# Two heads per maximum and exponential, and a shorter table of steps, in a four-layer attention and expert kernel on one core

## The reference

```python
x = _L0_conv_ref(x, ...)                     # one-head attention over 256 positions, 16 channels wide
x = x + _L1_conv_ref(_gn(x), ...)            # group norm, 8-head attention (16 channels each), projection
t = _to_tokens(x)
t = t + _L2_attn_ref(_ln_t(t))               # softmax(x x^T) x
t = t + _L2_ffn_ref(_ln_t(t), ...)           # 8 experts of 512, all of them, weighted by two probabilities
t = t + _L3_attn_ref(_ln_t(t), ...)          # 8 heads, RoPE, window of 32 keys back
t = t + _L3_ffn_ref(_ln_t(t), ...)           # shared expert and 2 of 8 routed experts of 64
```

## Time and profile before

| | us |
|---|---|
| median of 3 runs (lowest, highest) | 787.24 (785.09, 787.25) |
| the profiled execution | 783.05 |
| span of its trace | 781.3 |
| PE matmul busy | 633.1 (81%) |
| VectorE busy | 390.9 (50%) |
| ScalarE busy | 343.4 (44%) |
| GpSimd busy | 333.7 (43%) |

### The profile page before, as it was taken

The page is one execution under the profiler, slowest core; times in us unless marked ns, Lnnn a source line. Parts: engine busy times, 40 slices in busy tenths (PEclk is TensorE's granted clock), DMA queues, the critical chain, the costliest instruction groups (busy, mean ns, idle before and its releaser), DMA issues.

```text
span 781.3 us, 9513 instructions
## 1 busy us (share of the span) xinstructions
PE 633.1 (81%) x3266; PEld 324.7 (42%) x3266; DVE 390.9 (50%) x799; ACT 343.4 (44%) x544; POOL 333.7 (43%) x620
## 2 busy tenths in 40 slices
PE   7788988677888977887997869996689889757768
PEld 5565455444344442434443424442334344334422
DVE  3464441557375564674556385644675434531233
ACT  2423224136466465365455346653744634212222
POOL 2543411606174186696146685428671534200300
PEclk9997566789999999988999889999999999855789
DMA  6600000000000000000000000000000000000000
GB/s 211 146 1 1 1 1 1 0 1 1 1 0 1 1 1 1 1 0 0 2 0 2 0 1 0 1 1 1 0 0 1 1 1 14 13 1 1 0 14 13
DMA packets 10226, 8.59 MB, mean 11 GB/s; under 512 B 4026, under 2 KB 8132, under 8 KB 10180
## 3 DMA queue, kind: packets, MB, share of 16 engines
q1 hardware_dynamic: 10180, 8.00, 3.6%
HBM read 6.94 MB, written 1.05 MB: 10 GB/s over the span
## 4 chain that ended last, share of the span: by engine, by line
PE 51%; DVE 16%; POOL 14%; issue 10%; ACT 8%; DMA 0%; POOLq 0%; SPq 0%; DVEq 0%; ACTq 0%
PE bank L540 9%; PE bank L547 8%; POOL h_s L1278 4%; ACT ET L750 4%; DVE shiftpad L1015 4%; DVE z_s L1090 3%; POOL xn_l L1271 3%; PE bank L266 3%; PE bank L399 3%; PE bank L431 3%; PE bank L454 2%; PE bank L413 2%; PE bank L591 2%; PE bank L576 2%; PE bank L391 1%
## 5 line engine op out<-in xcount | busy, mean ns | idle before, releaser
L1090 DVE TENSOR_TENSOR z_s<-bank,PB 128x1024 f32<-128x1024 f32 x128 | 156.4, 1222 | 164.7 <-PE bank L540 162.6
L1278 POOL TENSOR_TENSOR h_s<-z_s 128x512 f32<-128x512 f32 x128 | 163.0, 1299 | 153.7 <-ACT z_s L809 135.4
L540 PE MATMUL bank<-XN_C,W 128*128 128x512 f32 x256 | 144.1, 646 | 34.3 <-DVE z_s L1090 33.7
L547 PE MATMUL bank<-h_s,W 128*128 128x512 f32 x256 | 145.3, 651 | 1.4 <-ACT y_s L816 1.0
L809 ACT ACTIVATE z_s<-z_s,b 128x1024 f32<-128x1024 f32 x128 | 137.2, 1141 | 11.0 <-DVE z_s L1090 10.8
L1015 DVE TENSOR_REDUCE shiftpad<-bank 128x2 f32<-128x512 f32 (+1 forms) x128 | 66.6, 583 | 53.9 <-PE bank L399 29.4
L540 PEld LDWEIGHTS bank<-XN_C,W 128*128 128x128 f32 x256 | 44.7, 199 | 101.8 <-DVE z_s L1090 79.3
L750 ACT ACTIVATE ET<-bank 128x512 f32<-128x512 f32 (+1 forms) x128 | 55.8, 522 | 57.0 <-PE bank L431 30.1
L1264 POOL TENSOR_SCALAR root_l<-mv_l 128x4 f32<-128x4 f32 x12 | 2.8, 232 | 168.8 <-DVE mv_l L1046 168.3
L547 PEld LDWEIGHTS bank<-h_s,W 128*128 128x128 f32 x256 | 44.5, 202 | 37.0 <-issue 31.4
L771 ACT COPY XN_C<-bank 128x512 f32<-128x512 f32 x16 | 9.4, 585 | 68.2 <-PE bank L266 68.1
(11 more groups left out here) (246 smaller groups left out, 961.3 us busy)
## 6 DMA issues: line engine op xcount, KB each, us to landing
W<-in_L_ffn_W_dram SPq DMA_DIRECT2D x1, 2048.0 KB, 8.7
XN_C<-in_x_dram SPq DMA_DIRECT2D x4, 256.0 KB, 3.0
out_dram<-z_s SPq DMA_DIRECT2D x4, 256.0 KB, 2.2
Wgate<-in_L_ffn_W_gate_dram SPq DMA_DIRECT2D x1, 256.0 KB, 4.2
Wup<-in_L_ffn_W_up_dram SPq DMA_DIRECT2D x1, 256.0 KB, 4.8
Wdown<-in_L_ffn_W_down_dram SPq DMA_DIRECT2D x1, 256.0 KB, 4.3
early<-in_L_conv_W_qkv_dram SPq DMA_DIRECT2D x1, 192.0 KB
early<-in_L_conv_Wd_dram SPq DMA_DIRECT2D x1, 64.0 KB, 1.9
```

Of the source, the lines that this page charges most:

```text
L540: nc.tensor.matmul(to[:, :], W1[:, f // 4, f % 4 * P:(f % 4 + 1) * P], XN_C[:, pair(g)], start=True, stop=True).then_inc(filled("u", t)[0], 1)
L547: ins = nc.tensor.matmul(bank[D_BANK][:, :], W2[:, f, :], h_s[:, t % H_RING, :], start=(f == 0), stop=(f == FT - 1)).then_inc(s_dn, 1)
L1090: nc.vector.tensor_tensor(z_s[:, t % Z_RING, :].rearrange("p (w n) -> p w n", w=2), content("u", t)[:, None, :].broadcast_to([P, 2, W]), P ...
L1278: nc.gpsimd.tensor_tensor(h_s[:, t % H_RING, :], z_s[:, t % Z_RING, 0:W], z_s[:, t % Z_RING, W:2 * W], ALU.add).then_inc(s_h, 1)
```

## The change

Banks 3 to 6 become one tensor `quad`, and banks 3 and 4 share one pair of semaphores, 5 and 6 another (`KEEPER`). S and T take both pairs before their first matmul (`take_two`) and report a pair when its second head is done. `highest` and `exps` handle a pair of heads in one instruction: 64 maxima and 64 exponentials in place of 128 and 128. There are two sets of offsets: in the expert turns (`SLOW`) S, MT, T, PV, OT stand at 0 and 2, 2 and 4, 4 and 6, 6 and 8, 9, and the second pair's maximum and exponential come a step later than the first's; outside the turns (`FAST`) at 0 and 1, 1 and 2, 1 and 2, 2 and 3, 4. Within a step PE now does MT and PV ahead of T. The turns begin at step 32, and the table has 203 steps instead of 224. In the steps before 32 the ring of banks 1 and 7 has bank 0 as a third member. `prepare_late` moves from s = 18 to s = 42, and the experts of group 2 now stand in steps 180 to 185, among the halves of images 14 and 15. The lines move: L540 is L561 in the changed kernel, L1090 is L1118, L1015 is L1042, L750 is L776, L399 is L420, L431 is L452, L454 is L475, L413 is L434, L355 is L376, L497 is L518, L516 is L537, L266 is L287.

```diff
-FF_AT = 36
+FF_AT = 32
-L0_AT = (0, 3, 6, 9)
-P1_AT = (8, 12, 30, 44)
-ATT_AT = (9, 13, 17, 21, 33, 41, 49, 57, 89, 97, 121, 129, 153, 161, 185, 189)
-TAIL_AT = (22, 30, 50, 66, 106, 138, 170, 198)
-L2_AT = (27, 37, 61, 77)
-SPREAD_AT = (35, 45, 69, 101)
+L0_AT = (0, 3, 10, 16)
+P1_AT = (7, 13, 22, 28)
+ATT_AT = (8, 10, 14, 16, 37, 45, 53, 61, 93, 101, 117, 125, 149, 157, 179, 181)
+TAIL_AT = (15, 21, 56, 72, 112, 136, 168, 186)
+L2_AT = (20, 26, 61, 77)
+SPREAD_AT = (30, 40, 72, 104)
-PREP_AT = tuple(FF_AT + FT * g + 45 for g in range(3)) + (177,)
-ROUTER_AT = (113, 145, 177, 205)
-EXPERT_AT = (172, 178, 200, 211)
-LAST = 224
-U_BANK, D_BANK, QUAD_BANK, MISC = (0,), 2, 3, (1, 7)
-XG_BANK, XU_BANK, XW_BANK = (0, 3), (4, 6), 5
+PREP_AT = (81, 109, 141, 172)
+ROUTER_AT = (118, 141, 173, 191)
+EXPERT_AT = (168, 174, 180, 196)
+LAST = 203
+U_BANK, D_BANK, QUAD_BANK, MISC, MISC_FIRST = 0, 2, 3, (1, 7), (1, 7, 0)
+KEEPER = (0, 1, 2, 3, 3, 5, 5, 7)
+SLOW = {"S": (0, 2), "MT": (2, 4), "T": (4, 6), "PV": (6, 8), "OT": 9, "later": 1}
+FAST = {"S": (0, 1), "MT": (1, 2), "T": (1, 2), "PV": (2, 3), "OT": 4, "later": 0}
+STEPS = [FAST if at < FF_AT or at > FF_AT + TURNS else SLOW for at in ATT_AT]
...
+        quad = ctx.enter_context(nc.psum_tensor("quad", [P, SLOTS, 512], F32))
...
+            def take_two(what, i, jj):
+                return fill(what, i, (QUAD_BANK + 2 * jj, QUAD_BANK + 2 * jj + 1))
...
-                to = [take("S", (i, j), QUAD_BANK + j) for j in range(SLOTS)] if a >= IMAGES else [None] * SLOTS
+                for jj in range(2):
+                    take_two("S", (i, jj), jj)
...
-                        if t == NT - 1:
-                            ins.then_inc(filled("S", (i, j))[0], 1)
+                        if t == NT - 1 and j % 2 == 1:
+                            ins.then_inc(filled("S", (i, j // 2))[0], 1)
...
-                    to = take("xg", (g, k), XG_BANK[k % 2])
+                    to = take("xg", (g, k), (0, QUAD_BANK)[k % 2 if g == GROUPS - 1 else 0])
-                    to = take("xu", (g, k), XU_BANK[k % 2])
+                    to = take("xu", (g, k), (1, 5)[k % 2] if g == GROUPS - 1 else None)
-                        to = take("xw", (g, k), XW_BANK)
+                        to = take("xw", (g, k), 7 if g == GROUPS - 1 else None)
...
-                for j in range(SLOTS):
-                    act.wait_ge(*filled("T", (i, j)))
-                    nc.scalar.activation(ET[:, i % 2 * SLOTS + j, 0:width(a)], content("T", (i, j))[:, 0:width(a)], ACT.Exp).then_inc(
-                        emptied("T", (i, j))[0], 1)
+                at = i % 2 * SLOTS + 2 * jj
+                act.wait_ge(*filled("T", (i, jj)))
+                nc.scalar.activation(ET[:, at:at + 2, 0:width(a)], quad[:, 2 * jj:2 * jj + 2, 0:width(a)], ACT.Exp).then_inc(emptied("T", (i, jj))[0], 1)
...
-                for j in range(SLOTS):
-                    dve.wait_ge(*filled("S", (i, j)))
-                    nc.vector.tensor_reduce(shiftpad[:, i % 2, :, j, HD], content("S", (i, j))[:, 0:width(a)].rearrange("p (t k) -> p t k", t=NT),
-                                            AX.X, ALU.max, negate=True).then_inc(emptied("S", (i, j))[0], 1)
+                at = slice(2 * jj, 2 * jj + 2)
+                dve.wait_ge(*filled("S", (i, jj)))
+                nc.vector.tensor_reduce(shiftpad[:, i % 2, :, at, HD].rearrange("p t j -> p j t"),
+                                        quad[:, at, 0:width(a)].rearrange("p j (t k) -> p j t k", t=NT),
+                                        AX.X, ALU.max, negate=True).then_inc(emptied("S", (i, jj))[0], 1)
...
-                if s == 18:
+                if s == FF_AT + 10:
                     prepare_late()
```

More of the change, by code:

```diff
@@ L249, in _, with fill @@
         def _(pe):
-            turns = [0]
+            turns, beat = {MISC: 0, MISC_FIRST: 0}, [0]
+            def fill(what, i, banks):
+                kept = KEEPER[banks[0]]
+                was = max(content_of[b] for b in banks)
+                if was:
+                    pe.wait_ge(bank_emptied[kept], was)
+                fills[kept] += 1
+                for b in banks:
+                    content_of[b] = fills[kept]
+                turn_of[what, i] = banks[0], fills[kept]
+                return bank[banks[0]]
             def take(what, i, b=None):
                 if b is None:
[L255 to L261, removed]
+                    ring = MISC if beat[0] >= FF_AT else MISC_FIRST
+                    turns[ring] += 1
+                    b = ring[turns[ring] % len(ring)]
+                return fill(what, i, (b,))
+            def take_two(what, i, jj):
+                return fill(what, i, (QUAD_BANK + 2 * jj, QUAD_BANK + 2 * jj + 1))
             def turn_tiles(what, i, source, to=None):
@@ L441, in values @@
                 i = a * 2 + half
-                for j in range(SLOTS):
-                    pe.wait_ge(*emptied("T", (i, j)))
+                for jj in range(2):
+                    pe.wait_ge(*emptied("T", (i, jj)))
                 if half == 0:
@@ L598, in _ @@
             for s in range(LAST):
+                beat[0] = s
                 for g in range(GROUPS):
@@ L605, in _ @@
                 for a in range(2 * IMAGES):
[L606 to L611 removed]
+                    for half in range(2):
+                        if s == ATT_AT[a] + STEPS[a]["MT"][half]:
+                            turn_shifts(a, half)
+                for a in range(2 * IMAGES):
+                    for half in range(2):
+                        if s == ATT_AT[a] + STEPS[a]["PV"][half]:
+                            values(a, half)
+                    if s == ATT_AT[a] + STEPS[a]["OT"]:
                         turn_o(a)
+                for a in range(2 * IMAGES):
+                    for half in range(2):
+                        if s == ATT_AT[a] + STEPS[a]["T"][half]:
+                            scores_turned(a, half)
                 for ap in range(2 * GROUPS):
@@ L618, in _ @@
                 for a in range(2 * IMAGES):
-                    k = s - ATT_AT[a]
-                    if k in (0, 2):
-                        scores(a, k // 2)
-                    if k in (1, 3):
-                        turn_shifts(a, k // 2)
+                    for half in range(2):
+                        if s == ATT_AT[a] + STEPS[a]["S"][half]:
+                            scores(a, half)
                 if 0 <= s - FF_AT - DOWN_LAG < TURNS:
@@ L1155, in _ @@
                 for a in range(2 * IMAGES):
-                    k = s - ATT_AT[a]
-                    if k == 8:
+                    for half in range(2):
+                        if s == ATT_AT[a] + STEPS[a]["MT"][half]:
+                            add_shift(a, half)
+                for a in range(2 * IMAGES):
+                    if s == ATT_AT[a] + STEPS[a]["OT"]:
                         scale_o(a)
@@ L1164, in _ @@
                 for a in range(2 * IMAGES):
-                    k = s - ATT_AT[a]
-                    if k in (0, 2):
-                        highest(a, k // 2)
-                    if k in (1, 3):
-                        add_shift(a, k // 2)
+                    for half in range(2):
+                        for jj in range(2):
+                            if s == ATT_AT[a] + STEPS[a]["S"][half] + jj * STEPS[a]["later"]:
+                                highest(a, half, jj)
                 for g in range(GROUPS):
```

85 lines of the change are left out of this document (40 added, 45 removed).

## The result

The changed kernel takes 804.36 us (median of 4 runs, 802.94 to 806.03) against 786.32 (785.09 to 787.25): 1.0231 times the time before, 95% interval 1.0204 to 1.0258. I had forecast 779 with a range of 762 to 802. Its profiled execution spans 802.8 us, 21.5 more than before.

The account below looks back on a forecast made before the run. It saw three stages with three limits: attention at half clock before and after the turns, PE in them. 15.8 - 15.2 - 8.5 = -8 us gave 775 against the profiled 783.05; 4.2 more for the median made 779, range 762 to 802.

Parts of the forecast that it names:

- The two-head instruction: On DVE and ACT: a two-head maximum takes 1.21 us, a two-head exponential 1.1 us.
- Before the turns, +15.8: Start to first turn: early start given back by longer halves, work moved ahead delays first turn; +15.8 us, ends -4 and +31.
- losing the early start: Before the turns: first S comes 10 us earlier, but serial halves over paired banks give the ten us back.
- The slower rival: Serial halves before the turns hold the clock at 1.2 GHz, 11.5 us a half; 799 us in all, chance 0.30.
- the faster rival: Layer 0 keeps the clock at 0.90 before the turns, 8.7 us a half; 763 us in all, chance 0.17.
- In the turns, -15.2: Expert turns: work moved ahead and waits for maxima go, image 4 adds 3 us; -15.2 us in sum.
- the -8 for the waits: Expert turns: PE's 8.8 us of waits for DVE's maxima nearly all go, since MT comes two steps after S; -8 us.
- What moved ahead is gone here: Expert turns: a projection (4.5 us) and a layer 2 (about 5.7) leave, image 4's two S and an MT add 3.
- Moving an attention of layer 3 changes nothing: Expert turns: moving an attention of layer 3 from group 1 to group 2 changes nothing in the sum.
- `prepare_late` costs nothing: Expert turns: it falls between two POOL batches and is hidden; if it does not fit, next batch up to 5 us late.
- After the turns, -8.5: Last turn to end: first S 5 us earlier, four halves 4.4 longer, 8 saved behind the output; -8.5 us, ends -14 and 0.
- "No change" as a rival: Expert turns: waits for the gate take in what the maxima give back, turns only 7 us shorter; 787 us, chance 0.10.

Follow-up runs that it names:

- e4: Changed kernel with layer 2 of group 1 and the projection of group 3 moved behind the first turns; 789.9 us, 1.006 times the kernel before.
- i1: Changed kernel's bank pairs and two-head instructions with the old table of steps and old attention offsets; 794.7 us, 1.013 times the kernel before.
- d1: Kernel before with only its start moved: layer 0 of groups 2 and 3 later, first projections and attentions earlier; 791.1 us, 1.007 times before.
- e8: Changed kernel with the old attention offsets in the expert turns alone; 802.6 us, 1.020 times the kernel before.
- n1: Changed kernel with spread offsets in the expert turns (MT 3 and 5, PV 7 and 9, OT 10); 789.7 us, 1.007 times the kernel before.
- c1: Changed kernel with the edits of e4, e5 and e8 together; 773.8 us, 0.985 times the kernel before.
- c2: Changed kernel with the edits of e4, e5 and n1 together; 770.2 us, 0.980 times the kernel before.
- e1: Changed kernel with two layer norms moved off the expert norms they stood right behind on POOL; 805.2 us, 1.023 times the kernel before.
- c3: c2 with the two layer norms moved off the expert norms as in e1; 768.7 us, 0.977 times the kernel before.
- e5: Changed kernel with the experts of group 2 behind the last attention again (step 187 instead of 180); 799.7 us, 1.020 times the kernel before.
- e2: Changed kernel with images 4 to 7 started four steps earlier and their tails at 51 and 67; 840.9 us, 1.070 times the kernel before.

## Why the prediction was wrong

**The two-head instruction: right.** 1.220 us measured for 1.21, 1.021 for 1.1.

**Before the turns, +15.8: right in size, partly in its reasons.** First S 35.57 (35.9), a half 10.2 us (10, but without the projection of group 1, which I counted apart), layer 2 of group 0 at 125.7 (128.4), first `ff_up` at 178.45 (177.4). e4 shows the larger part: what was put ahead of the first turn costs it 19 us. The reason given for losing the early start, the pairs, is one of two (i1), the mixing with layer 0 the other (d1). The slower rival, halves at 11.5 us with all of it at 1.2 GHz, came in i1, where nothing stands among the halves (12.2 us at 0.50). It did not come in the changed kernel, which has layer 0 among them: 36 to 128 ran at 0.78, where the same stretch had 0.71 before, and 799 us was near the result for another cause. Nor did the faster rival come, with 8.7 us a half. Of the oscillation that the Trainium skill tells of, in "TensorE: Matmul & The Clock Gate", "A second HAM failure mode: psum-queue depth-cycling", these means show no loss against before; whether the clock oscillated between the halves, they cannot say.

**In the turns, -15.2: wrong, and this decides.** The step that failed is the -8 for the waits; the -10.2 was oversized besides. Three terms stood in it.

- "The waits for maxima nearly all go: -8." Most did go, 8.8 to 2.2, and e8 with its old offsets has 3.8. But I took a wait that vanishes for time that is gained, and did not ask what bounds the turn then. The offsets that took the waits away put MT, S, T and PV all into every second step; e8 and n1 show that this costs 8.5 us against the old offsets and 17.4 against spread ones. The sign of this term was wrong: with what I expected of it, it is off by some 16 us.
- "What moved ahead is gone here: -10.2, and +3 for image 4." e4 measures 3.8 between its two places, e8 and c1 2.4 with the old offsets, n1 and c2 10.4 with the spread ones. In the changed kernel the first turns have nothing beside them and run as the bare chain at a clock of 0.50, 3.39 us each (gates at 184.02, 187.41 and 190.81), so little of it came out.
- "Moving an attention of layer 3 changes nothing", and no word of the norms' new places. PE's waits for xn_l went from 8.0 to 18.4 us, and with the old table in i1 they are 8.4, so the new places bring them. e1 and c3 show that moving two of these norms gains nothing, since other waits grow (in e1 xn_l falls to 14.1 us, and the wait for `early`, L1029, rises from 4.4 to 8.5). What the norms cost in all stays open.

With the first two terms as measured (+8.5 and about -4) some 4.5 us of the 9.0 remain. In e8, which has the new table with the old offsets, groups 0 to 3 differ from before by -6.7, -0.2, +5.4 and +1.9 us, so they lie in groups 2 and 3; their cause was not isolated, and the norms are the nearest candidate.

That `prepare_late` costs nothing was right. POOL in the changed kernel:

```profile
217.80 0.36 POOL L1232 MEMSET early<- 128x320 f32 x1
...
230.67 9.89 POOL L1308 TENSOR_TENSOR h_s<-z_s 128x512 f32<-128x512 f32 x8 [1.65 <-ACT z_s L834]
```

It begins at 217.80, right behind two products, and the next product (230.67) still stood idle for 1.65 us waiting for ACT, so it held up nothing.

**After the turns, -8.5 (its terms give -8.6): right in sign, -4.5.** First S 8.0 us earlier after the last gate (forecast 5), the time behind the output 10.5 shorter (8), but the halves 13.9 longer where I had 4.4: 14.1 us each instead of 11.7. e5 shows that the blocks among them are the cause: without them the same halves take 10.2 us. The terms that I listed for a half add up to 9.7 at full clock and 13.1 at half, not to the 10.4 and 12.5 that I wrote; what a half measured lies above all of these, so the blocks were the term that I sized too small.

**"No change" as a rival** had the gate's wait take in what the maxima gave back. The wait did grow, by 9.4 us, but the reason I gave, many short slips, was not it: it is in the main the odd steps standing empty, for the same wait is 32.8 us in e8 and 36.4 in n1.

## What to carry to other kernels

Where a loop's turn has a shortest time set by a hand-off between two engines, the spare room is in every turn, and here small pieces were free when they stood one to a turn and lost that room when they stood together in every second one; ask of a wait that is taken away what the turn is bound by afterwards. Before merging instructions over several buffers, look at what their separate release lets overlap. And moving a piece of one engine's list can drop it into another engine's batch: hold its new place against every batch, as e2 shows for ACT's tables.

## What the runs showed that was not expected

Matmuls of heads that lie in different rows of the array overlap, four in turn more than two: 8.2 us of PE busy for the same work that takes 15.3 with two in turn. The bare chain of `ff_up` and gate ran at 1.2 GHz: granted clock 0.50 from 178 to 210, with PE busy 24.97 of 31.60 us. Ahead of it PE had waited 8.89 us for POOL's norm, to 176.57 us, and the clock had fallen in that wait (1.00 from 160 to 171 us, 0.50 from 172 to 176.5). In the kernel before, with attention and layer 2 beside the turns from the start, group 0 had 0.98. Which of the two, the wait ahead or the bare chain, kept the clock low is not shown.
